# Ordering the partial products of a split-precision matmul so that the low half of x comes last

## The reference

```python
x = x + conv(x, W0, taps=9, groups=4) + (cond @ c_weight0.T + side)      # layer 1
x = x + einsum('boi,bih->boh', agg_w(cond), x) + agg_b(cond)             # layer 2
x = x + einsum('boi,bih->boh', agg_w(cond), x) + agg_b(cond)             # layer 3
x = x + conv(x, W3, taps=9, groups=4) + (cond @ c_weight3.T + side)      # layer 4
```

## Time and profile before

| | |
|---|---|
| median of 3 runs | 2595.03 us (2594.97 to 2595.71) |
| the profiled execution | 2595.53 us, of which the span 2593.7 us |
| granted TensorE clock, mean | 0.996 of full speed |
| TensorE busy | 2554.3 us, 98% of the span, 11082 matmuls |
| VectorE busy | 2279.6 us, 88% |
| ScalarE busy | 2074.5 us, 80% |
| moved by DMA | 808.77 MB, mean 312 GB/s |

### The profile page before, as it was taken

How to read it: one execution, slowest core, us unless ns; L and a number is a source line. 1 busy time by engine, 2 the same in 40 slices (tenths; PEclk the granted TensorE clock), 3 DMA queues, 4 the chain that set the end, 5 groups by cost and what they waited for, 6 DMA issues and landing times.

```text
span 2593.7 us, 38318 instructions
## 1 busy us (share of the span) xinstructions
PE 2554.3 (98%) x11082; PEld 2070.0 (80%) x11082; DVE 2279.6 (88%) x3386; ACT 2074.5 (80%) x1938; POOL 3.7 (0%) x17
## 2 busy tenths in 40 slices
PE   6999999999999999999999999999999999999998
PEld 4788888888888888888888888888888888888886
DVE  8988888888888888888888888888888888888885
ACT  4788878888887888788888878888887888888785
POOL 0000000000000000000000000000000000000000
PEclk9999999999999999999999999999999999999999
DMA  5788888888888888888888888888888888888876
GB/s 197 278 317 316 320 321 315 316 324 317 315 321 321 318 316 321 319 312 321 324 317 315 320 319 312 321 324 316 317 319 320 312 320 324 317 315 320 320 299 235
DMA packets 335449, 808.77 MB, mean 312 GB/s; under 512 B 37066, under 2 KB 40146, under 8 KB 302674
## 3 DMA queue, kind: packets, MB, share of 16 engines
q1 hardware_dynamic: 333200, 807.16, 83.6%
q10 hardware_dynamic: 2242, 1.53, 0.2%
HBM read 137.45 MB, written 134.22 MB: 105 GB/s over the span
## 4 chain that ended last, share of the span: by engine, by line
PE 97%; DVE 1%; DMA 1%; ACT 0%; issue 0%; SPq 0%; ACTq 0%
PE pair L821 82%; PE quad L865 14%; PE pair L855 1%; DMA x_ch<-x_ph 0%; DVE mixed L642 0%; DMA x_in<-in_x 0%; PE quad L802 0%; DVE weighted L630 0%; DVE w_hi L575 0%; DVE x_ch L616 0%; SPq L278 0%; ACT x_ch L375 0%; ACT x_out L504 0%; PE pair L814 0%; DVE x_hi L674 0%
## 5 line engine op out<-in xcount | busy, mean ns | idle before, releaser
L821 PE MATMUL pair<-x_hi,w_hi 128*128 128x512 f32 x3072 | 1227.0, 399 | 5.0 <-issue 3.3
L821 PE MATMUL pair<-x_hi,w_lo 128*128 128x512 f32 x3072 | 1213.1, 395 | 0.0
L821 PE MATMUL pair<-x_lo,w_hi 128*128 128x512 f32 x3072 | 1209.0, 394 | 0.0
L821 PEld LDWEIGHTS pair<-x_hi,w_lo 128*128 128x128 f32 x3072 | 579.5, 189 | 137.3
L821 PEld LDWEIGHTS pair<-x_lo,w_hi 128*128 128x128 f32 x3072 | 581.5, 189 | 131.4
L821 PEld LDWEIGHTS pair<-x_hi,w_hi 128*128 128x128 f32 x3072 | 578.6, 188 | 133.3 <-issue 4.9
L642 DVE TENSOR_REDUCE mixed<-weighted 128x128 f32<-128x1152 f32 x256 | 576.9, 2254 | 0.1
L375 ACT COPY x_ch<-x_in 128x1024 f32<-128x1024 f32 x256 | 530.5, 2074 | 2.0 <-DMA x_in<-in_x 2.0
L434 ACT COPY x_ph<-pair 128x512 f32<-128x512 f32 x512 | 314.7, 615 | 270.9 <-PE pair L821 270.9
L426 ACT COPY x_out<-x_ch 128x1024 f32<-128x1024 f32 x252 | 522.7, 2074 | 0.3 <-DMA x_ch<-x_ph 0.3
L442 ACT ACTIVATE x_ph<-pair,bias_now 128x512 f32<-128x512 f32 x508 | 355.3, 699 | 208.7 <-PE pair L821 208.7
(11 more groups left out here) (84 smaller groups left out, 614.6 us busy)
## 6 DMA issues: line engine op xcount, KB each, us to landing
x_ph<-x_ch SPq DMA_DIRECT2D x1024, 256.0 KB, 2.6
x_ch<-x_ph SPq DMA_DIRECT2D x1024, 256.0 KB, 2.6
x_in<-in_x SPq DMA_DIRECT2D x128, 1024.0 KB, 5.5
out<-x_out SPq DMA_DIRECT2D x128, 1024.0 KB, 4.2
x_out<-in_W SPq DMA_DIRECT2D x8, 144.0 KB, 5.4
expert<-in_e ACTq DMA_DIRECT2D x2, 512.0 KB, 8.0
x_ph<-in_e_t SPq DMA_DIRECT2D x1, 512.0 KB, 4.5
x_ph<-in_small ACTq DMA_DIRECT2D x1, 458.5 KB, 3.6
```

Source lines behind the costliest of these rows:

```text
L821: mm = nc.tensor.matmul(conv_bank[g % 2], w[l][:, m, g, :], x[:, g, m:m + N], start=(m == 0 and x is hi and w is w_hi), stop=(m == BLK - 1 ...
```

## The change

In `conv` the loops change places. The nine matmuls of a group were ordered by block (for each block high by high, high weights by low x, low weights by high x). Now they are ordered by product: high by high for all three blocks, low weights by high x for all three, and high weights by low x for all three. A group no longer waits for x's low part before its first matmul, but for the high part there, and for the low part before its seventh. In `middle` the three matmuls of a phase are ordered in the same way, with a wait for the high part before the first and one for the low part before the third.

```diff
-            def conv(l, g, hi, lo, done):
-                for m in range(BLK):
-                    for w, x in ((w_hi, hi), (w_hi, lo), (w_lo, hi)):
+            def conv(l, g, hi, lo, lo_ready, count, done):
+                for w, x in ((w_hi, hi), (w_lo, hi), (w_hi, lo)):
+                    if x is lo:
+                        pe.wait_ge(lo_ready, count)
+                    for m in range(BLK):
                         mm = nc.tensor.matmul(conv_bank[g % 2], w[l][:, m, g, :], x[:, g, m:m + N],
                                               start=(m == 0 and x is hi and w is w_hi),
-                                              stop=(m == BLK - 1 and w is w_lo))
+                                              stop=(m == BLK - 1 and x is lo))
                 mm.then_inc(done, 1)
             def conv1(b, groups=range(G)):
-                pe.wait_ge(x_lo_ready, b + 1)
+                pe.wait_ge(x_hi_ready, b + 1)
...
-                    conv(0, g, x_hi, x_lo, conv1_done)
+                    conv(0, g, x_hi, x_lo, x_lo_ready, b + 1, conv1_done)
             def conv4(b, groups=range(G), after_x4=False):
-                    pe.wait_ge(x3_split, G * b + g + 1)
+                    pe.wait_ge(x3_high, G * b + g + 1)
...
-                    conv(1, g, x3_hi, x3_lo, conv4_done)
+                    conv(1, g, x3_hi, x3_lo, x3_split, G * b + g + 1, conv4_done)
             def middle(b):
                 for q in range(PH):
-                    pe.wait_ge(x1_split, PH * b + q + 1)
-                    for m, x in ((m_hi, x1_hi), (m_hi, x1_lo), (m_lo, x1_hi)):
+                    pe.wait_ge(x1_high, PH * b + q + 1)
+                    for m, x in ((m_hi, x1_hi), (m_lo, x1_hi), (m_hi, x1_lo)):
+                        if x is x1_lo:
+                            pe.wait_ge(x1_split, PH * b + q + 1)
                         mm = nc.tensor.matmul(mid_bank[:, q, :], m[:, :], x[:, q, :],
-                                              start=(m is m_hi and x is x1_hi), stop=(m is m_lo))
+                                              start=(m is m_hi and x is x1_hi), stop=(x is x1_lo))
                     mm.then_inc(mid_done, 1)
```

## The result

| | before | after |
|---|---|---|
| median | 2595.08 us (19 runs, 2594.66 to 2595.71) | 2599.51 us (19 runs, 2598.58 to 2602.18) |
| ratio | | 1.0019, 95% interval 1.0013 to 1.0026 |
| profiled span | 2593.7 us | 2597.7 us |

The changed kernel is 4.4 us slower. The forecast was 2593.6, a little faster.

What follows compares the result with a forecast made beforehand. TensorE, busy 98% of the span, was taken as the bound. Profiled execution 2595.53 us - 0.94 (start) - 0.5 (end) = 2594.1; the median, 0.5 under the profiled one, gives 2593.6 us, range 2588.5 to 2600.

Steps and rivals of the forecast that it cites:

- Part 1: Loop: low halves are ready 2.1 to 3.8 us early, so relaxing their waits removes nothing in 125 passes: 0 us.
- Part 2: Groups and phases: 1536 added waits, carried by weight loads, cost 0 us; upper ends 9 us, or 123 without overlap.
- Rival B: Slower, chance 0.15: an added wait inside a group costs weight-load time; 2599.7 us at 0.004 us each, 2602.8 at 0.006.
- Part 3: Convolutions: no neighbours share weights any more; taken as 0 us, with ends of -8 and +8 us.
- the sign of being wrong: Loop: the prediction is wrong if the period moves by over 0.04 us or loop matmuls wait for VectorE.
- Rival C: Faster, chance 0.10: the pace depends on which operands are neighbours, and 7.8 us go: 2585.8 us.
- Part 4: Start: conv4(0) begins on x3's high half, 0.94 us sooner, and the shift passes through to the end: -0.94 us.
- The clock term: Start, after conv4(0)'s wait: half-rate stretch costing 1.7 us, left as is; -1.7 if the clock does not fall, +1.7 if twice.
- Part 5: End: the last block's middle layer starts sooner, then low halves limit it; the gain stays to the end: -0.5 us.

Runs made afterwards that it cites:

- experiment 2: Kernel before with its old matmul order but the change's split waits, the low one ahead of a group's second matmul: 2594.66 us, ratio 0.9998.
- experiments 6 and 10: First: kernel before, convolutions by block with low x last, 2590.84 us. Second: separate kernel, six orders with TensorE alone or beside partners; by block 16.94, by product 16.90 us.
- experiments 16 and 17: Fastest order (by block, low x last) with split waits: first, all x and weight tiles at one residue modulo 256 bytes, 2591.59 us; second, also weights shifted m elements, 2593.04.

## Why the prediction was wrong, step by step

*Part 1, the waits in the loop: right.* TensorE waits for nothing there before or after.

*Part 2, the added waits: right.* I took 0 for 1536 waits; experiment 2 has them all at an unchanged 19.76 us. Rival B named 2599.7 us and the measured time is 2599.5, but by a mechanism that this run excludes: its number is luck.

*Part 3, the order itself: this step failed.* I took 0 with -8 and +8 us as ends; it was 19.813 - 19.760 = 0.053 us per pass, 6.7 us over 125 passes, and so the period moved by more than the 0.04 us that I had set as the sign of being wrong. The end was wide enough, the value taken was not. What the runs show in its place is a price of the sequence of addresses: with tiles of 528 elements the same change of order made the kernel 20 us faster (2602.8 to 2582.6) instead of 4.4 slower. Rival C had the pace depend on neighbours, but by shared weights and as a saving; experiments 6 and 10 exclude that.

Two things were wrong in how I came to 0. I set the ends by a difference of busy times, 399 against 394 ns, and read it as a saving or a price of neighbours with the same weights. The rows after have the same 399 and 395 ns with no such neighbours left:

```profile
L825 PE MATMUL pair<-x_hi,w_hi 128*128 128x512 f32 x3072 | 894.6, 399 | 4.5 <-issue 2.7
...
L825 PE MATMUL pair<-x_lo,w_hi 128*128 128x512 f32 x3072 | 880.8, 395 | 0.0
```

So they say nothing of the order. And I took "the same within 0.01 us" as a reason for 0, although 0.01 us is 4% of an interval and the effect is 0.3%: 0.0006 us of each of 84 intervals. A row with that step can't exclude 6.7 us in 10,752 matmuls; the period over many passes can't either, since it says nothing of an order that isn't in the trace.

*Part 4, the start: right in the wait that counts, wrong in the other end.* -0.94 was -0.77. But I had both ends of the wait before conv4(0) move by about 1 us and the wait stay at 3 to 4 us. TensorE's last matmul before it had started at 64.83 and now starts at some 64.6, so the wait shrank from 3.25 to 2.72 us. The clock term that I left in place for that reason went away in the profiled execution (-1.6), inside the bounds given.

*Part 5, the end: right.* -0.5 was -0.40, with the slower pace of some 120 matmuls in it.

*The chances.* Forecast and rivals gave "slower by over 0.2%" 0.11; the result is 0.19% slower, just inside what I called no change.

## What to carry to other kernels

When TensorE is 98% busy and never waits, splitting a wait gains only at the two ends, and an edit of the matmul sequence can weigh more: six orders of nine matmuls spread the pass by 0.4% (19.727 to 19.813 us), and with the tiles' width by 0.7% (19.680 to 19.820). One window repeated had 226.7 or 236.7 ns with where it lay. Compare the period of the loop before and after first: it shows such a shift to a nanosecond and tells it from waits. And try tile pitches together with the order: here one pitch (528 in place of 514 elements) was worth more, 17 us, than anything in the waits.

## What the runs showed of the hardware that I had not expected

- A met wait carried by a weight load has no measurable price: 12 more per pass, the pass unchanged at 19.760 us.
- The interval of matmuls of one shape, with full clock, depends on the addresses of moving windows and weights modulo 256 bytes: 226.7 ns for a window at the weights' own place, 236.7 ns one element off, and 233.3 ns for a window 64 bytes before the weights. Two sequences that are equal modulo 256 bytes had intervals equal to 0.01 ns. Data (real or zero) and load by VectorE, ScalarE and DMA changed nothing to 0.02 ns in the mean, one PSUM bank for two nothing to 0.04 ns.
- Every pass measured is a whole multiple of 6.667 ns (19.760, 19.813, 19.787, 19.727, 19.767, 19.680, 19.820 and 19.733 us). The single intervals are not. And what came before takes part in them: in the kernels of experiments 16 and 17 the middle layer has the same tiles at the same addresses and the same order, and yet takes 2.746 us in one and 2.768 in the other. Why stays open.
